# Token attention of a hybrid block on one Trainium2 core: the exponentials become the moving operand and the values the stationary one, in three 32-column strips

## The reference, cut to what matters

```python
def _L2_attn_ref(x, qkv_w, proj_w, proj_b, temperature):
    qkv = (x @ qkv_w.T).reshape(B, N, 3, H, Dh)
    qkv = jnp.transpose(qkv, (2, 0, 3, 1, 4))
    q, k, v = (qkv[0], qkv[1], qkv[2])
    attn = jnp.einsum('bhnd,bhmd->bhnm', q, k) / C ** 0.5
    attn = attn / temperature
    attn = jnp.where(diag, -jnp.inf, attn)
    attn = jax.nn.softmax(attn, axis=-1)
    out = jnp.einsum('bhnm,bhmd->bhnd', attn, v)
    out = jnp.transpose(out, (0, 2, 1, 3)).reshape(B, N, C)
    return out @ proj_w.T + proj_b

def _L3_attn_ref(x, w_qkv, w_proj, b_proj):
    ...
    scores = jnp.where(causal[None, None], scores, jnp.float32(-jnp.inf))
    weights = jax.nn.softmax(scores, axis=-1)
    out = jnp.einsum('bhqk,bhkd->bhqd', weights, v)
    return out.transpose(0, 2, 1, 3).reshape(B, T, C) @ w_proj + b_proj

t = t + _L2_attn_ref(_ln_t(t), ...);  t = t + _L2_ffn_ref(_ln_t(t), ...)
t = t + _L3_attn_ref(_ln_t(t), ...);  t = t + _L3_ffn_ref(_ln_t(t), ...)
```

## Time and profile before

| what | value |
|---|---|
| median of three runs | 1125.0 us (1124.26 to 1126.78) |
| profiled execution, span from first to last instruction | 1127.2 us |
| TensorE busy | 958.1 us, 85% of the span |
| VectorE, ScalarE, GpSimd busy | 51%, 39%, 31% |
| `weighted_values` (line 1016), both layers | 1344 matmul instructions, 161.7 us busy |

### The profile page before, as it was taken

The page is one execution under the profiler, slowest core; times in us unless marked ns, Lnnn a source line. Parts: engine busy times, 40 slices in busy tenths (PEclk is TensorE's granted clock), DMA queues, the critical chain, the costliest instruction groups (busy, mean ns, idle before and its releaser), DMA issues. The chain is left out here.

```text
span 1127.2 us, 19914 instructions
## 1 busy us (share of the span) xinstructions
PE 958.1 (85%) x6512; PEld 845.9 (75%) x6512; DVE 573.5 (51%) x1736; ACT 437.1 (39%) x698; POOL 352.6 (31%) x386
## 2 busy tenths in 40 slices
PE   1787777689983799999979999957999997999998
PEld 1655555389982599888869999936888886888887
DVE  5766565320044477666435656434766753444442
ACT  1243434320022334443255455522344333555453
POOL 4223323290003222331143533432234134233432
PEclk9986887679985799999979999966999997999999
DMA  3700000000102434322000000014343410000000
GB/s 71 109 12 0 0 0 0 1 4 15 15 1 46 87 80 86 82 63 64 1 1 0 0 0 0 1 42 91 91 91 72 93 26 1 9 7 13 8 7 15
DMA packets 28969, 36.76 MB, mean 33 GB/s; under 512 B 10696, under 2 KB 25856, under 8 KB 28928
## 3 DMA queue, kind: packets, MB, share of 16 engines
q1 hardware_dynamic: 28928, 36.24, 15.6%
HBM read 25.06 MB, written 11.17 MB: 32 GB/s over the span
## 5 line engine op out<-in xcount | busy, mean ns | idle before, releaser
L1413 PE MATMUL ps<-w,ff_b_h 128*128 128x96 f32 x1536 | 181.8, 275 | 6.7 <-ACT ff_b_fT L1469 6.7
L1413 PEld LDWEIGHTS ps<-w,ff_b_h 128*128 128x128 f32 x1536 | 178.5, 192 | 10.5 <-issue 7.3
L1480 ACT ACTIVATE ff_b_h<-ps,b 128x512 f32<-128x512 f32 x192 | 128.8, 687 | 121.5 <-PE ps L1405 121.3
L1016 PE MATMUL ps<-values,at_b_pT 128*128 128x102 f32 x1344 | 161.7, 276 | 1.0 <-POOL at_b_pT L941 0.4
L1016 PEld LDWEIGHTS ps<-values,at_b_pT 128*128 128x128 f32 x1344 | 155.2, 192 | 3.3 <-issue 1.4
L941 POOL TENSOR_SCALAR_AFFINE_SELECT at_b_pT<-at_b_pT 128x768 f32<-128x768 f32 x64 | 54.6, 865 | 237.3 <-ACT at_b_pT L1126 236.6
L1553 DVE SCALAR_TENSOR_TENSOR tok<-ps,ff_b_gate,tok 128x96 f32 (+1 forms) x224 | 56.0, 312 | 136.1 <-PE ps L1413 136.1
L1189 DVE TENSOR_REDUCE at_b_mf<-ps 128x6 f32<-128x1536 f32 (+1 forms) x64 | 98.1, 1552 | 25.5 <-PE ps L993 25.0
L614 DVE SCALAR_TENSOR_TENSOR ca_qk<-ca_raw,dw,ca_qk 96x225 f32<-96x225 f32 (+1 forms) x256 | 98.8, 451 | 0.0
L1126 ACT ACTIVATE at_b_pT<-ps 128x1536 f32<-128x1536 f32 x64 | 80.9, 1291 | 43.7 <-PE ps L1001 43.5
L991 PE MATMUL ps<-keys,at_b_qs 96*128 96x256 bf16 (+1 forms) x384 | 70.8, 272 | 22.6 <-issue 20.0
(11 more groups left out here) (224 smaller groups left out, 1557.8 us busy)
## 6 DMA issues: line engine op xcount, KB each, us to landing
at_parts<-at_b_part SPq DMA_DIRECT2D x96, 96.0 KB
at_b_qs<-at_parts SPq DMA_DIRECT2D x16, 288.0 KB, 4.2
keys<-at_parts SPq DMA_DIRECT2D x16, 288.0 KB, 5.4
at_b_qs<-at_parts SPq DMA_DIRECT2D x16, 192.0 KB, 5.8
keys<-at_parts SPq DMA_DIRECT2D x16, 192.0 KB, 6.3
w<-in_L_ffn_w SPq DMA_DIRECT2D x4, 576.0 KB
chan<-in_x SPq DMA_DIRECT2D x4, 384.0 KB, 5.5
windows<-lines_d SPq DMA_DIRECT2D x96, 13.0 KB, 1.6
```

Of the source, the lines that this page charges most:

```text
L1016: ins = nc.tensor.matmul(ps[:, 6 + u, OW * t:OW * (t + 1)], pT[:, u, k, h, P * t:P * (t + 1)], vp[:, slot, u, k, h, :], start=(n == 0), st ...
L1413: ins = nc.tensor.matmul(ps[:, 6 + e % 2, C * t:C * (t + 1)], h[:, e % 2, j, P * t:P * (t + 1)], f.w2[:, e * HC + j, :], start=(j == 0), s ...
L1480: nc.scalar.activation(h[:, e % 2, j, :], ps[:, 3 * (e % 2) + j, :], ACT.Gelu, bias=f.b1[:, e * HC + j:e * HC + j + 1]).then_inc(s_h, 1)
```

## The change

The roles of the two operands of `weighted_values` are exchanged. The stationary operand is now the values of one head, 128 keys by 32 columns (16 of values, 16 of ones), and the moving operand is a tile of the exponentials, 128 keys by up to 256 queries. Three heads write to three strips of 32 partitions of PSUM, the other three to the same strips further on in the bank. The result stands with features on partitions, so ScalarE copies it to SBUF (`keep_out`, into `oV`) and TensorE turns it back in four transposes (`turn_back`); from there VectorE's division and the rest go on as before. A burst of `weighted_values` is now one tile of keys instead of one tile of queries, and has 6 products instead of 12 (layer 3 before: 6 and 12). The array of values is 32 columns wide and is set to ones by one memset instead of one and eight. The places of several calls are changed:

```diff
-VD = D + 1
+VD = 2 * D
+HR = 3
...
-    m.vp = sb("values", [P, 2, 2, TPI, H, OW])
+    m.vp = sb("values", [P, 2, 2, TPI, H, VD])
...
-                def weighted_values(i, slot, u, t):
-                    if t == 0:
-                        pe.wait_ge(s_zero, 4 * i + 2 * u + 2)
-                    terms = [(k, h) for k in range(1 if causal and t == 0 else TPI) for h in range(H)]
-                    for n, (k, h) in enumerate(terms):
-                        ins = nc.tensor.matmul(ps[:, 6 + u, OW * t:OW * (t + 1)], pT[:, u, k, h, P * t:P * (t + 1)],
-                                               vp[:, slot, u, k, h, :], start=(n == 0), stop=(n == len(terms) - 1))
-                    if t == TPI - 1:
+                def weighted_values(i, slot, u, k):
+
+                    pe.wait_ge(s_zero, 4 * i + 2 * u + k + 1)
+                    n0 = P if causal and k == 1 else 0
+                    for h in range(H):
+                        r, q = h // HR, h % HR
+                        ins = nc.tensor.matmul(ps[VD * q:VD * (q + 1), 6 + u, N * r + n0:N * (r + 1)], vp[:, slot, u, k, h, :],
+                                               pT[:, u, k, h, n0:N], start=(k == 0 and r == 0), stop=(k == TPI - 1 and r == 1),
+                                               skip_group_check=True)
+                    if k == TPI - 1:
                         ins.then_inc(s_O, 1)
+
+                def turn_back(i, u):
+                    pe.wait_ge(s_ev, 2 * i + u + 1)
+                    for t in range(TPI):
+                        for r in range(2):
+                            ins = nc.tensor.transpose(ps[:, 6 + u, C * (2 * t + r):C * (2 * t + r + 1)],
+                                                      oV[:, u, r, P * t:P * (t + 1)], m.ident[0:C, 0:C])
+                    ins.then_inc(s_B, 1)
...
                     scores(i, slot, 0, 0)
                     if back:
-                        turn_out(i - 1, 0)
+                        turn_back(i - 1, 0)
                     pe.wait_ge(s_vp, 2 * i + 2)
                     scores(i, slot, 0, 1)
                     if back:
-                        project(i - 1, 0)
                         weighted_values(i - 1, 1 - slot, 1, 0)
+                        turn_out(i - 1, 0)
+                        weighted_values(i - 1, 1 - slot, 1, 1)
                     pe.wait_ge(s_mx, 4 * i + 1)
                     scores(i, slot, 1, 0)
                     if back:
-                        pe.wait_ge(s_tk, 2 * i - 1)
+                        project(i - 1, 0)
                     pe.wait_ge(s_mx, 4 * i + 2)
                     scores(i, slot, 1, 1)
+                    if back:
+                        turn_back(i - 1, 1)
+                        pe.wait_ge(s_tk, 2 * i - 1)
                     turn_maxima(i, 0)
-                    if back:
-                        weighted_values(i - 1, 1 - slot, 1, 1)
                     pe.wait_ge(s_mx, 4 * i + 3)
                     pe.wait_ge(s_mr0, i + 1)
                     transposed_scores(i, slot, 0, 0)
...
+                def keep_out(i, u):
+                    act.wait_ge(s_O, 2 * i + u + 1)
+                    nc.scalar.copy(oV[:, u, :, :].rearrange("c r n -> c (r n)"), ps[0:C, 6 + u, :]).then_inc(s_ev, 1)
...
                     weights(i, 1)
+                    keep_out(i, 0)
                     if ahead == 2:
                         parts(i + 2)
+                    if ahead:
+                        keep_out(i, 1)
                     out(i, 0)
...
                 def out(i, u):
-                    dve.wait_ge(s_O, 2 * i + u + 1)
+                    dve.wait_ge(s_B, 2 * i + u + 1)
...
                     maximum(i, 0, 0)
                     if back:
-                        add(i - 1, 0)
+                        out(i - 1, 0)
                     maximum(i, 0, 1)
                     maxima_parts(i, 0)
                     maximum(i, 1, 0)
+                    if back:
+                        add(i - 1, 0)
                     maximum(i, 1, 1)
...
                     values(i + 1, 1 - slot)
-                    out(i, 0)
                     maxima(i + 1, 1 - slot)
```

More of the change, by code:

```diff
@@ L29 @@
 H, D = 6, 16
-VD = D + 1
+VD = 2 * D
+HR = 3
 MAX_ROWS = 3 * H
-OW = H * VD
 Q = 4 * P
@@ L807, in attention_constants @@
     link(pool.memset(m.mxp[:, :, :, :], 0.0))
[L808 to L812, removed]
+    link(pool.memset(m.vp[:, :, :, :, :, :], 1.0))
 def token_rstd(m, pool, i, n, s_rstd, s_mv=None):
@@ L862, in token_attention @@
     (s_own, s_xn, s_T, s_xT, s_qk, s_p1, s_r1, s_p2, s_p3, s_v, s_vp, s_S, s_mx, s_mp, s_M, s_mr0, s_mr1, s_ST, s_ex, s_O, s_rc,
-     s_on, s_OT, s_oT, s_pr, s_tk, s_st, s_mv, s_rstd, s_part) = (sem(f"at_{n}") for n in (
+     s_on, s_ev, s_B, s_OT, s_oT, s_pr, s_tk, s_st, s_mv, s_rstd, s_part) = (sem(f"at_{n}") for n in (
          "pool_own", "normed", "normed_turned", "xT", "qk", "part1", "rest1", "part2", "part3", "v", "v_kept", "scores",
-         "max", "max_parts", "max_turned", "max_rows0", "max_rows1", "scoresT", "exp", "out", "recip", "out_normed", "out_turned", "outT",
+         "max", "max_parts", "max_turned", "max_rows0", "max_rows1", "scoresT", "exp", "out", "recip", "out_normed", "out_kept", "out_back", "out_turned", "outT",
          "proj", "tok", "stats", "mv", "rstd", "parts_stored"))
@@ L888, in token_attention @@
         rec = sb("rec", [P, 2, TPI, H])
+        oV = sb("oV", [C, 2, 2, N])
         on = sb("on", [P, 2, TPI, C])
@@ L1101, in _ @@
                 weighted_values(end - 1, 1, 1, 0)
+                turn_back(end - 1, 0)
+                weighted_values(end - 1, 1, 1, 1)
                 turn_out(end - 1, 0)
-                weighted_values(end - 1, 1, 1, 1)
+                turn_back(end - 1, 1)
                 project(end - 1, 0)
@@ L1138, in step @@
                     weights(i, 1)
+                    keep_out(i, 0)
                     if ahead == 2:
                         parts(i + 2)
+                    if ahead:
+                        keep_out(i, 1)
                     out(i, 0)
+                    if not ahead:
+                        keep_out(i, 1)
                     if ahead:
@@ L1179, in values @@
                         for t in range(TPI):
[L1180 to L1183, removed]
+                            ins = nc.vector.tensor_copy(vp[:, slot, u, t, :, 0:D],
+                                                        ps[:, 3 * u + 1, C * t:C * (t + 1)].rearrange("p (h d) -> p h d", d=D))
                         ins.then_inc(s_vp, 1)
@@ L1209, in out @@
                 def out(i, u):
-                    dve.wait_ge(s_O, 2 * i + u + 1)
-                    o = ps[:, 6 + u, 0:TPI * OW].rearrange("p (t h w) -> p t h w", t=TPI, h=H)
+                    dve.wait_ge(s_B, 2 * i + u + 1)
+                    o = ps[:, 6 + u, 0:TPI * H * VD].rearrange("p (t h w) -> p t h w", t=TPI, h=H)
                     nc.vector.reciprocal(rec[:, u, :, :], o[:, :, :, D]).then_inc(s_rc, 1)
```

## The result

The changed kernel takes 1179.1 us in the median (1175.6 to 1179.7), against 1125.9 before; the ratio is 1.046 (1.0436 to 1.0483). It is slower by 53 us, for the reason foreseen and by somewhat less than forecast.

The account below looks back on a forecast made before the run. TensorE was taken to bound both attentions. From 1127 us profiled, +42 for twelve steps and -3 at the ends gave +39, the clock +36: 1202; the median lies 2.2 lower, so 1200 us, range 1158 to 1255.

Parts of the forecast that it names:

- The sign: Whole kernel: the change makes it slower, by 6.7%, with chance 0.94 for slower.
- The pause: TensorE idles ahead of the first scores, twelve times, as ScalarE's copy holds up the casts: 5.2 and 4.7 us.
- The two lost covers: Bursts no longer hide the row copy (+1.6 us a step) and the last exponential (+0.7 in layer 2).
- The clock: TensorE's granted clock at 0.50 for 6.0 us of work behind each pause: +3.0 us a step, +36 in all.
- Rivals 1: In the bursts, strips run one after another, 2.6 us a burst: time 1250 us, chance 0.17.
- 4 (the clock stays up): TensorE's granted clock does not fall in the attention loops: 36 us less, time 1164 us, chance 0.10.
- 5 (no pause): On ScalarE the casts go through before the copy, so TensorE does not idle: time 1104 us, faster, chance 0.05.
- twelve steps without the clock: Looped attention steps before any fall of the clock: +3.4 us each in layer 2, +3.5 in layer 3, +42 together.
- ends of the layers and the rest: Four last steps at about -1.5 us each, each layer's end about 1.4 longer: -3 us.
- The bursts: TensorE's weighted values: 1.51 us a burst instead of 2.69 in layer 2; -4.8 us a step there, -3.6 in layer 3.
- rival 2: In the bursts, three strips stream at once, 0.87 us a burst: time 1180 us, chance 0.12.
- rival 3: TensorE's array empties at each change between strips and full width, 0.16 us each, 20 us: time 1220 us, chance 0.13.

Follow-up runs that it names:

- e1: Changed kernel with ScalarE's casts of parts(i + 2) again ahead of the copy keep_out(i, 0): 1123.0 us, ratio to before 0.9965.
- e2: Changed kernel with TensorE's second burst of image 0 directly behind the first, ahead of the queries and keys; ScalarE's order as changed: 1136.2 us, ratio 1.0055.
- e5: Kernel before with one wait added: ScalarE's parts(i + 2) in the loop wait for at_out of image 0: 1209.7 us, ratio 1.0733.
- e3: Changed kernel with 16 more float32 products by the identity, result unread, ahead of the first scores: 1157.9 us, ratio 1.0292.
- e9: Changed kernel with the second burst of every image written to the first strip for all six heads: 1217.8 us, ratio to before 1.0792.

## Why the prediction was right, and where it was off

The sign, the place and the mechanism hold. The pause is where it was put, ended by what was named, twelve times; e1 and e2 shorten it in two independent ways, to 1.8 and 2.8 us in layer 2, and take back 56 and 43 us; e5 makes the loss without any of the rest. The two lost covers are there: 1.52 to 1.61 us for the row copy against 1.6, and 1.23 for the exponentials against 0.7. The clock falls behind each pause. Rivals 1 (the strips take turns), 4 (the clock stays up) and 5 (no pause) are out.

The sizes were off, in directions that partly cancel:

| term | predicted | measured |
|---|---|---|
| a burst of 256 columns | 1.51 us | 1.0 us |
| a burst of 128 columns | 0.76 us | 0.57 us |
| eight transposes back | 0.84 us a step | 0.7 us at full clock (0.34 for four) |
| the pause | 5.2 and 4.7 us | 4.2 to 4.6 us |
| the wait for the exponentials | 0.7 us (layer 2) | 1.23 us |
| twelve steps without the clock | +42 us | about +26 us, by the steps of e3 at full clock |
| the clock | +36 us | about +30 us, of which e3 takes back 21 |
| ends of the layers and the rest | -3 us | -9 us, 4 of them ahead of the attention |
| time | 1200 us | 1179 us |

The burst of 128 columns and the transposes, in layer 3 at full clock, each with what TensorE starts behind it:

```profile
836.28 0.64 PE L1014 MATMUL ps<-at_b_pT,values 128*32 128x128 f32 x12
836.85 0.23 PE L988 MATMUL ps<-keys,at_b_qs 96*128 96x128 bf16 x1
...
839.42 0.50 PE L1024 MATMUL ps<-ident,at_b_oV 96*128 96x96 f32 x4
839.76 0.28 PE L1005 MATMUL ps<-ident_b,maxima 128*114 128x128 bf16 x2
```

The step that failed is in "The bursts": I let the second instruction of a product run beside the first of the next and no more, since they follow each other in the queue. All three strips stream at once, which was rival 2 (0.87 for the burst); its 1180 us is the nearest number. The 1.0 is 0.87 and 0.13 on top. Between 453.50 and 453.85 two transposes take 0.35 us, where they took 0.21 between scores, so each change between strips and full width seems to cost about 0.14; 128 of them would be 18 us, an estimate. That fits rival 3, which had 0.16 and 20 us: rival 2 is shown, and rival 3 fits beside it. The Trainium skill (TensorEngine Tiling (Array Packing), Key Properties) says that a change of tiling mode drains TensorE; the 0.14 us agree with it, though no run took the changes away. The Trainium skill's factor for three column tiles of 512 columns, 2.38 (TensorE: Matmul & The Clock Gate, Part 3, Measured speedup), compares with 2.6 here for 256 columns in float32 (e9), and was closer than my 1.7 (2.6 us over 1.51).

The wait for the exponentials grew just as the burst shrank: a faster burst in front of a wait is not a gain. The pause of layer 2 was about 1 us shorter, 0.6 of it because VectorE's second kind of parts took 1.29 us instead of 1.91 (below). The clock cost 1.9 us a step in layer 2 instead of 3.0, since only 4.6 us of dense work lay in the low stretch, not 6.0: part of that stretch lay inside the pause. In layer 3 it cost 3.1 a step, at 0.81 over five steps. There it falls a second time in each step from 868 us on, behind the row copy's wait that ends at 867.66 (0.50 over 868.80 to 875.60), which the prediction did not count. How much of this is due to the pause before it and how much to that wait was not tested.

## What to carry to other kernels

A new instruction on an in-order engine makes everything behind it wait for its input: put it behind whatever the bound engine needs next, or make its input earlier. What a long operation hides is lost when it gets faster, so look at what ends next to it before counting its gain. In these runs a pause of TensorE was paid a second time in the clock of the work behind it, and the same work cost more there; so it paid to close the waits, or even to fill them.

## What the runs showed that I had not expected

VectorE and GpSimd were slower where some of their instructions ran beside each other. VectorE's two bfloat16 parts in the kernel before, and GpSimd's normalization beside them:

```profile
439.16 1.91 DVE L1173 TENSOR_TENSOR at_b_part<-at_b_rest,at_b_part 96x512 bf16<-96x512 f32 x2
```

```profile
439.36 1.17 POOL L832 TENSOR_TENSOR at_b_xn<-tok,mv 128x384 f32 x1 [0.37 <-POOL rstd L824]
440.71 1.04 POOL L836 TENSOR_TENSOR at_b_xn<-at_b_xn,rstd 128x384 f32<-128x384 f32 x1 [0.19 <-POOL at_b_xn L832]
```

In the changed kernel GpSimd is done before VectorE gets there: the same two take 1.29 us instead of 1.91 (446.31, above), and GpSimd's two

```profile
443.83 0.83 POOL L828 TENSOR_TENSOR at_b_xn<-tok,mv 128x384 f32 x1 [0.37 <-POOL rstd L820]
444.85 0.82 POOL L832 TENSOR_TENSOR at_b_xn<-at_b_xn,rstd 128x384 f32<-128x384 f32 x1 [0.19 <-POOL at_b_xn L828]
```

0.83 and 0.82 instead of 1.17 and 1.04. It comes and goes with the overlap: in e1, where the parts run early again and beside GpSimd, the two take 2.03 us, and in e5, the kernel before with late parts, 1.29. But not every overlap does it: GpSimd's instruction at 444.85 runs beside VectorE's first parts at 444.94, which read one operand from PSUM, and both keep their time (0.82, and 1.28 for two). That the overlap is the cause was not tested by itself.

One result was expected and still deserves a second look: a single wait in the program, taken twelve times in a kernel that was otherwise full, cost 83 us (e5).
